# Two-layer kernel in three woven columns: the scan's front moved a batch ahead, the rest's chain reordered

## The chip, the cores and the metric

One core of one Trainium2 chip. The time is the device time of one launch in microseconds, the median of the runs shown.

## What is computed

Two layers of a mixed network on x of 8 batches x 512 tokens x 256 features, in float32. Every part is added to its input.

```python
x = x + scan_layer(layernorm(x))      # state space: in_proj, conv of 4 taps, silu, softplus, 16 states
x = x + ffn_layer(layernorm(x))       # attention only modulates a gated MLP of 1024
x = x + gla_layer(layernorm(x))       # gated linear attention, 4 heads, chunks of 64
x = x + moe_layer(layernorm(x))       # top 4 of 32 experts, inner size 96

# scan_layer, per batch; d over 512 channels, n over 16 states
h, gate = split(z @ in_proj_w); u = silu(conv(h) + b)
dt, B, C = split(u @ x_proj_w); dt, B, C = rms(dt), rms(B), rms(C)
dt = softplus(dt @ dt_proj_w + b)
s[t] = exp(dt[t] * A) * s[t-1] + dt[t] * u[t] * B[t];   y[t] = sum_n s[t] * C[t]
return ((y + u * D) * silu(gate)) @ out_proj_w

# ffn_layer, with its own rms norms of z
mod = 0.1 * tanh(attention(rms(z)) @ A)
g = silu(h @ W_in.T + mod * (h @ A) @ B);  return z + (g * (h @ W_up.T)) @ W_down

# gla_layer
gk = log_sigmoid(z @ Wgk1 @ Wgk2 + b) / 16        # decays, cumulated inside each chunk
o = q_g @ k_g.T (lower triangle) @ v + q_g @ state;  o = o / rms(o) * w * silu(z @ Wg);  return o @ Wo
```

## The kernel before, in words

The kernel is written engine by engine. Each engine has one in-order queue, and parts of the work are generators that yield between small steps. `weave` (line 151) takes steps of two generators in turn, by hand-laid run lengths, the table `ORDER` for batches 0 to 6 and the table `LAST` for the end. So the order of the work on each engine is fixed in the program, and engines meet by semaphores.

**The two columns.** `scan_part(turn, late)` is the whole state-space layer of a batch. `rest_part(turn)` is everything from the feed-forward layer to the linear attention of a batch. `scan_part(t+1)` is woven with `rest_part(t)`. `rest_part(t+1)` starts when the last `out` of `scan_part(t+1)` has been added to `xa`. Routing of the expert layer for batch t-1 (`late_*`) sits inside `scan_part(t+1)`. Before the first rest, `scan_part(0)` runs alone.

**The scan part.** Its front: `x` is loaded into `xa`, statistics (`norm_stats`, line 1292), normalised `xn`, transposed (`T`), projected (`hid`, `gate`), convolved (line 1321: one tap on ACT, three on DVE, from a copy with three zero columns), silu to `u`, `ssm` products, root of sums on POOL, transposes `dtT` and `bcT`, then `dtp` and a softplus from Abs, Relu, Exp and Ln. The B and C rows go to `bc_dram` and come back spread over all partitions, two states a load. After the front 32 units follow (two states of one channel tile each): ACT makes two decays (line 1097), DVE multiplies the drive (`drive_unit`, line 1399), scans (line 1367), multiplies with C (line 1376), and PE sums over the states by transposes (line 2047) into bank 0 or 1. `y_of` adds the skip and the gate, `out` is the output product. All banks of this part are 0 and 1 (ring `A`).

**The rest part.** Statistics of `xa` (`mv0`), POOL makes `rs` and from it `rs2`, ACT writes `nrm` and from it `zn`; transposes `zT`, products `q`, `k`, `v`; 22 score units `S` whose maxima DVE takes (line 1541); maxima transposed (`nmT`) and added to `qT`; 16 score blocks `ST` with their exponentials on ACT (line 1144) and products with v into banks 6 and 7 (`D`); `OT`, `oT`, `mod`, `hA`; eight MLP steps (`mlp_tile`, `down`) with weights streamed into three slots `wslot`, sums in `D`; `add_down`, statistics `mv1`, `gn`, `nT`, then the linear attention: `low`, `gk`, `gq`, `gkey`, `gv`, `gg`, the cumulated decay `cs` (line 1600), `qg`, `kg`, `kd` (line 1614), `kdT`, seven state updates `dS` (lines 1623, 1628), four masked products `AT` (line 1635), four outputs `GO`, sums `g_ss` (line 1640), root on POOL, `goT`, `gout` (line 1657), statistics `mv2`, and `mn`, the rows that are routed. Banks 2 to 5 (ring `B`).

**The end.** Beside the last rest run 40 expert blocks; after it the others and the sums.

## Time and profile before

| | |
|---|---|
| median of 3 runs (lowest, highest) | 3019.35 us (3016.56, 3025.76) |
| span of the profiled execution | 2958.7 us |
| instructions | 36517 |
| PE busy | 2351.0 us (79%) |
| DVE busy | 2163.5 us (73%) |
| ACT busy | 1383.5 us (47%) |
| POOL busy | 575.3 us (19%) |

Busy time is the union of an engine's instructions; where they overlap they are counted once, so that mean durations times counts come out larger. PEclk is the granted clock of TensorE as a share of 2.4 GHz. A line of the busy time by stage or period has the window, its length in us, the busy us and instructions (x) of PE, PE's weight loads, DVE, ACT and POOL, then the granted clock, the DMA engines' busy share and GB/s. A period is the time from one last add of `out` to `xa` (line 1387) to the next.

### The profile page before, as it was taken

The page shows a single profiled execution, that of the slowest core. Times are in us where ns is not written, and L with a number is a line of the kernel's source. Part 1 is how long each engine was busy: PE and PEld are TensorE (multiplying, and loading weights), DVE is VectorE, ACT ScalarE, POOL GpSimd, SP SyncE. Part 2 cuts the span into 40 slices and gives each one's busy share as a digit, 9 for nine tenths or more (in the row PEclk, how much of TensorE's full clock was granted, in tenths as well). Part 3 has the DMA queues.
Part 4 walks back from the last instruction along what each step waited for, and adds up shares of the span by engine and source line. Part 5 has one row for each costly group of instructions (what it writes and reads, how often), then busy time and mean ns, then how long its engine had stood idle before and what let it go on. Part 6 is the DMA issues. An engine that isn't in the chain of part 4 may idle for free. (4 is left out here: it accounts for less than half of the span.)

```text
span 2958.7 us, 36517 instructions
## 1 busy us (share of the span) xinstructions
PE 2351.0 (79%) x12305; PEld 1420.5 (48%) x12305; DVE 2163.5 (73%) x3017; ACT 1383.5 (47%) x2217; POOL 575.3 (19%) x569
## 2 busy tenths in 40 slices
PE   4448896889778977887788869787879688988991
PEld 2335354535453545444544545345535453556880
DVE  4993898489948894899669975998589852246666
ACT  5323654366535663566356634654465424143440
POOL 4000101120131013111311120212120230025661
PEclk8558897899889987998799979998999789988995
DMA  2320231023201321133113311231033182355757
GB/s 105 120 79 8 103 113 57 15 87 128 74 28 60 128 94 35 42 126 107 42 35 109 117 49 42 92 127 56 8 112 121 60 212 97 103 195 174 219 180 302
DMA packets 136229, 292.85 MB, mean 99 GB/s; under 512 B 14288, under 2 KB 79200, under 8 KB 135792
## 3 DMA queue, kind: packets, MB, share of 16 engines
q1 hardware_dynamic: 122224, 251.96, 26.2%
q0 software_dynamic: 13824, 38.55, 3.6%
q8 instruction: 104, 1.70, 0.2%
q14 instruction: 77, 0.63, 0.1%
HBM read 220.91 MB, written 69.54 MB: 98 GB/s over the span
## 5 line engine op out<-in xcount | busy, mean ns | idle before, releaser
L1367 DVE TENSOR_TENSOR_SCAN scan<-scan 128x1024 f32<-128x1024 f32 x256 | 585.9, 2289 | 34.4 <-ACT scan L1097 26.4
L2047 PE MATMUL bank<-ident,scan 128*128 128x128 f32 x2048 | 325.3, 315 | 168.9 <-DVE scan L1376 158.1
L1097 ACT ACTIVATE scan<-scan 128x511 f32<-128x511 f32 x512 | 337.2, 713 | 164.2 <-DVE scan L1367 163.5
L2047 PEld LDWEIGHTS bank<-ident,scan 128*128 128x128 f32 x2048 | 271.6, 162 | 260.1 <-DVE scan L1376 158.4
L1399 DVE TENSOR_TENSOR scan<-scan 128x1024 f32<-128x1024 f32 x256 | 310.5, 1213 | 29.5 <-PE bank L2047 28.5
L1376 DVE TENSOR_TENSOR scan<-scan 128x1024 f32<-128x1024 f32 x256 | 312.0, 1219 | 7.8 <-DVE rest L1579 7.5
L1936 PE MATMUL bank<-hT,wslot 128*128 128x512 f32 x512 | 246.9, 607 | 0.0
L1541 DVE TENSOR_REDUCE rest<-bank 128x2 f32<-128x1024 f32 (+3 forms) x176 | 196.5, 1126 | 66.5 <-PE bank L2118 63.5
L819 POOL DMA_INDIRECT rows_dram<-stage,slot_at x128 | 164.9, 1288 | 370.4 <-DVE scan L1367 313.1
L1144 ACT ACTIVATE rest<-bank 128x2048 f32<-128x2048 f32 (+3 forms) x128 | 158.2, 1236 | 146.7 <-PE bank L2138 146.6
L1936 PE MATMUL bank<-xT,scan 128*128 128x512 f32 (+1 forms) x352 | 185.0, 672 | 7.4 <-ACT xT L983 4.8
L2113 PE MATMUL bank<-rest 32*128 32x384 f32 (+3 forms) x1024 | 185.4, 464 | 2.3 <-DVE rest L1541 1.7
L1321 DVE SCALAR_TENSOR_TENSOR scan<-scan 128x512 f32<-128x512 f32 x96 | 71.9, 752 | 144.9 <-ACT scan L1033 142.4
L983 ACT ACTIVATE scan<-bank 128x512 f32<-128x512 f32 x112 | 65.2, 595 | 230.1 <-PEq L2052 89.5
L1936 PE MATMUL bank<-scan 128*128 128x512 f32 x320 | 153.2, 608 | 3.6 <-ACT scan L983 3.1
L797 POOL TENSOR_SCALAR rs<-mv 128x4 f32<-128x4 f32 x24 | 10.1, 421 | 691.9 <-DVE off L1300 691.9
L1936 PEld LDWEIGHTS bank<-hT,wslot 128*128 128x128 f32 x512 | 88.8, 189 | 115.4 <-issue 108.6
L1923 PE MATMUL bank<-ident,rest 128*128 128x128 f32 x352 | 57.8, 324 | 107.5 <-ACT rest L1110 52.6
L2135 PE MATMUL bank<-causal_t,ident_b 128*128 128x128 bf16 x512 | 54.8, 235 | 105.5 <-ACT rest L1144 67.7
L894 POOL DMA_INDIRECT y_dram<-rest,y_at x120 | 115.1, 959 | 60.6 <-DVE rest L1867 47.5
L2071 PE MATMUL bank<-wslot,rest 128*128 128x256 f32 x512 | 120.4, 380 | 1.0 <-PE bank L2047 0.2
L1163 ACT ACT_TABLE_LOAD x49 | 62.9, 1283 | 120.7 <-PE bank L1936 120.6
(341 smaller groups left out, 4231.2 us busy)
## 6 DMA issues: line engine op xcount, KB each, us to landing
scan<-bc_dram SPq DMA_DIRECT2D x256, 512.0 KB, 3.8
wslot<-wt SPq DMA_DIRECT2D x64, 384.0 KB, 3.5
rows_dram<-pad SPq DMA_DIRECT2D x32, 670.0 KB
scan<-y_dram SPq DMA_DIRECT2D x32, 512.0 KB, 10.1
rest<-rows_dram SPq DMA_DIRECT2D x108, 134.0 KB, 2.5
scan<-rows_dram SPq DMA_DIRECT2D x52, 134.0 KB, 2.7
scan<-wt SPq DMA_DIRECT2D x4, 1536.0 KB, 13.6
xa<-x SPq DMA_DIRECT2D x8, 512.0 KB, 3.8
```

The lines of the kernel that those rows point to most:

```text
L819: g.indirect_dma_start(rows_dram, bass.IndirectOffsetOnAxis(ap=slot_at[:, j:j + 1], axis=0), stage[:, j % NT], None).then_inc(scattered.se ...
L894: g.indirect_dma_start(y_dram, bass.IndirectOffsetOnAxis(ap=y_at[:, b % NYA:b % NYA + 1], axis=0), y[:, n % y.shape[1]], None).then_inc(y_ ...
L1097: i = a.activation(decay[:, unit % 2, n, 1:], dt[:, c, 1:], ACT.Exp, scale=a_neg[:, c, 2 * pair + n:2 * pair + n + 1])
L1144: a.activation(probT[:, u % NPT, :, 0:SEQ - j * P], banks(("ST", u))[:, :, 0:SEQ - j * P], ACT.Exp)\
L1367: d.tensor_tensor_scan(flat, decay[:, unit % 2].rearrange("p n t -> p (n t)"), flat, 0.0, ALU.mult, ALU.add).then_inc(decay_used.sem, 1)
L1376: d.tensor_tensor(drive[:, unit % NDRIVE], drive[:, unit % NDRIVE], bc[:, load % 2, 1], ALU.mult).then_inc(unit_done.sem, 1)
L1399: d.tensor_tensor(drive[:, unit % NDRIVE], dtu[:, c].unsqueeze(1).broadcast_to([P, 2, SEQ]), bc[:, load % 2, 0], ALU.mult).then_inc(drive_ ...
L1541: d.tensor_reduce(nmax[:, t, heads, r].rearrange("p i r -> p r i"), banks(("S", u))[:, :, 0:n * width].rearrange("p r (i k) -> p r i k", i=n),
L1936: m = t_.matmul(b[0:rows, cols], lhsT, rhs, start=(i == 0), stop=(i == len(pairs) - 1))
L2047: m = t_.matmul(A.bank(("yT", c))[:, t * P:(t + 1) * P], drive[:, unit % NDRIVE, n, t * P:(t + 1) * P], ident[:, :], is_transpose=True, st ...
L2071: m = t_.matmul(D[t // 2][:, (t % 2) * HID:(t % 2 + 1) * HID], inner[:, f % 2, t * P:(t + 1) * P], slot[:, 2 * NF * P:], start=(first and ...
L2113: t_.matmul(b[:, k, at:at + width], qT[rows, i, t * P:(t + 1) * P], kT[rows, i, 0:width], start=(i == heads.start), stop=False, skip_group ...
```

## The change

The work of both columns is cut anew into three columns on each engine, `U` (the 32 units and `y`), `R` (the rest), `X` (everything at the side). `weave` takes steps from all three by one long run list per engine. `LAST` goes; `ORDER` covers the whole run up to the last experts.

- The scan's front is split. `front_part(t+2)` (statistics to the first two softplus tiles) is in X and runs beside `units(t+1)` and `rest_part(t)`. `gate_part` has the other two softplus tiles and the gate products. `out_part` has `out`. `tail_part` has `mv2` and `mn`. X is, on PE: out(t), gates(t+1), routing(t-1), front(t+2).
- Front, gates, out and routing use banks 6 and 7 (rings `F`, `G`, `O`, `K`) in turns with the rest, which has them for `D`. The front's `x`, `ssm` and two softplus tiles are in the weight slots, so is the routing's scratch. `handed` waits for the last holder of a bank. x is loaded twice, once for the front and once for the residual.
- `u` of channel tiles 2 and 3 has two places, for odd and even batches. The convolution is done by DVE in place, from PSUM. `y` is formed in `u` and `sgate`.
- In the rest: `rs2` comes straight from the variance and `zn` straight from `xa`; `nrm` and `hT` follow after the first transposes. `Wgk1 @ Wgk2` is folded once at the start, so `low` goes. `hA` and `up` of f = 0 stand before `mod`. `e_kd` and `kd` come before `qg` and `kg`. `dS`, `AT` and `GO` are interleaved as `CHUNK_WORK` says. The root of the sums, and the products with it, go token tile by token tile.

In the DVE list of the changed kernel a middle batch reads so (steps decoded from the run list; t is the rest's batch, the units are those of t+1, C is the product with C):

```
rest: statistics of xa              tail of t-1; units: scans 2-5; xb; drive 6, scan 6, drive 7, C 6
routing of t-1, first half          maxima 0, 1; rank; maxima 2, 3; rank; maxima 4, 5
scan 7 ... C 9 one step between each two maxima up to 21; dtu 2, scan 10; nmT 0-3
units drive 11 ... scan 20, y 0, y 1; OT 0-3; units to C 21; gmod; scan 22
inner 0-3; unit steps with inner 4, 5, 6, 7; scan 27, drive 28
add_down, mv1; front t+2: statistics; units C 27 ... scan 30; front: conv 0, 1; unit; conv 2, 3
cs; scan 31; kd; C 31; qg; kg; y 2; dS 0-2, AT 0; y 3; front: ssm; dS, AT, to AT 3
front: dt 0, dtu 0, dt 1; drive 0 of t+2; dS 6, g_ss 0, 1; dtu 1; out; go; scan 0; ... gout
```

The core of the diff:

```diff
-def weave(rest, scan, runs):
-    for n, part in zip(runs, itertools.cycle((rest, scan))):
-        for _ in range(n):
-            next(part, None)
+def weave(columns, order):
+    for run in order.split():
+        for _ in range(int(run[1:])):
+            next(columns[run[0]], None)
...
+CHUNK_WORK = [("dS", 0), ("dS", 1), ("dS", 2), ("AT", 0), ("dS", 3), ("AT", 1), ("GO", 0), ("dS", 4), ("AT", 2),
+              ("dS", 5), ("AT", 3), ("GO", 1), ("dS", 6), ("GO", 2), ("GO", 3)]
...
+            def front_in(turn):
+                yield
+                if turn >= 2:
+                    sp.wait_ge(down_done.sem, down_done.at(turn - 2, NFT))
...
+                sp.dma_start(x_f, x[turn:turn + 1].rearrange("b (t p) d -> p (b t) d", p=P)).then_inc(x_in.sem, 16)
...
+                    elif f == 0 and in_slots(turn - 1):
+                        sp.wait_ge(lv.sem, lv.named(turn - 1, "routed"))
                     sp.wait_ge(down_done.sem, down_done.at(turn, f - NSLOT + 1 if f >= NSLOT else max(g for g in range(NWT) if g % NSLOT == f) + 1 - NWT))
                     sp.dma_start(wslot[:, f % NSLOT, :], wt[f]).then_inc(w_in[f % NSLOT].sem, 16)
...
+                s = power(rp, turn, rs2[:, :], mv[:, :, 1], 1.0 + 1e-6, 1e-11, NT)
+                pool.wait_ge(rp.sem, rp.at(turn, s))
+                marked("off2", rp.step(g.tensor_tensor(off2[:, :], off[:, :], rs2[:, :], ALU.mult).then_inc(rp.sem, 1)))
...
+                        i = d.scalar_tensor_tensor(tile[:, back:], b[:, 0:SEQ - back], conv_w[:, c, k:k + 1], tile[:, back:], ALU.mult, ALU.add)
...
+            def front_part(turn):
+                yield
+                pe.wait_ge(fa.sem, fa.named(turn, "xn"))
+                if turn >= 2:
+                    pe.wait_ge(d_free.sem, d_free.at(turn - 1, 0))
...
+            def out_part(turn):
+                yield
+                pe.wait_ge(uv.sem, uv.named(turn, f"y{NCT - 1}"))
+                if turn + 1 < BATCH:
+                    handed(F.given_back(turn + 1, ("dtp", 0)), F.given_back(turn + 1, ("dtp", 1)))
...
-                product(B, turn, ("low", 0), [(g_gk1[:, c], xT[:, c]) for c in range(NF)], rows=RANK)
-                yield
-                pe.wait_ge(B.freed_sem(("low", 0)), B.freed_at(turn, ("low", 0)))
-                product(B, turn, ("gk", 0), [(gk2[:, :], lowT[0:RANK, :])])
+                product(B, turn, ("gk", 0), [(g_gkw[:, c], xT[:, c]) for c in range(NF)])
...
+            def side():
+                for turn in range(-1, BATCH):
+                    yield from out_part(turn) if turn >= 0 else idle(IDLE["PE"]["O"])
+                    if turn < BATCH - 1:
+                        yield from gate_part(turn + 1)
+                        yield from late_alone(turn - 1, turn - 1, K) if turn >= 1 else idle(IDLE["PE"]["L"])
+                        yield from front_part(turn + 2) if turn + 2 < BATCH else idle(IDLE["PE"]["F"])
...
+            columns = {
+                "U": itertools.chain.from_iterable(units(turn) for turn in range(BATCH)),
+                "R": itertools.chain(idle(IDLE["PE"]["R"]), *(rest_part(turn) for turn in range(BATCH)), late_alone(0, BATCH - 1, L)),
+                "X": side(),
+            }
+            weave(columns, ORDER["PE"])
```

## Rows read from the trace of the kernel before

**Rows 1.** Busy time by stage of the third rest, 844.3 to 1145.3.

```profile
844.30:884.70 40.40, 32.85 (x120) 19.72 (x120) 12.60 (x38) 19.72 (x37) 5.77 (x12) 0.83 0.04 14
884.70:938.00 53.30, 45.94 (x244) 22.72 (x243) 44.14 (x68) 27.64 (x44) 8.34 (x7) 0.98 0.15 49
938.00:990.00 52.00, 42.67 (x400) 21.08 (x400) 46.51 (x39) 32.37 (x38) 8.87 (x7) 0.89 0.32 110
990.00:1056.70 66.70, 65.57 (x243) 36.23 (x244) 63.69 (x53) 40.97 (x51) 1.14 (x1) 1.00 0.37 127
1056.70:1145.30 88.60, 60.84 (x322) 42.08 (x321) 74.27 (x86) 37.72 (x63) 23.32 (x15) 0.79 0.18 63
```

**Rows 2.** The same view by period, and the last stretch.

```profile
0.00:234.00 234.00, 106.35 (x400) 77.33 (x400) 176.67 (x153) 79.62 (x126) 31.00 (x64) 0.63 0.28 96
234.00:537.00 303.00, 252.03 (x1323) 144.62 (x1324) 232.81 (x243) 159.32 (x234) 29.53 (x28) 0.88 0.21 70
...
844.30:1151.60 307.30, 254.17 (x1352) 147.10 (x1353) 243.94 (x290) 160.49 (x237) 51.17 (x46) 0.89 0.22 76
...
2380.30:2690.00 309.70, 267.68 (x1365) 154.61 (x1366) 118.00 (x332) 105.03 (x193) 60.05 (x68) 0.91 0.52 154
```

**Rows 3.** DVE in order of time, two scan steps: start, us, engine, line.

```profile
404.94 2.29 DVE L1367 TENSOR_TENSOR_SCAN scan<-scan 128x1024 f32<-128x1024 f32 x1 [0.31 <-DVE rest L1579]
...
409.40 2.29 DVE L1367 TENSOR_TENSOR_SCAN scan<-scan 128x1024 f32<-128x1024 f32 x1
```

**Rows 4.** The same view, milestones of the third rest, 856 to 1145 us.

```profile
856.42 1.41 DVE L1294 BATCH_NORM_STATS2 a_stats<-xa 128x6 f32<-128x256 f32 x4 [3.91 <-DMA xa<-x]
...
942.01 0.69 DVE L1351 TENSOR_TENSOR scan<-scan 128x512 f32<-128x512 f32 x1
...
1093.26 0.68 DVE L1614 TENSOR_TENSOR rest<-rest 128x512 f32<-128x512 f32 x1
...
1115.32 1.42 DVE L1635 TENSOR_TENSOR rest<-bank,tri 128x256 f32<-128x256 f32 x4
...
1123.31 0.39 DVE L1640 TENSOR_REDUCE g_ss<-hT 128x4 f32<-128x256 f32 x1
...
1144.64 0.69 DVE L1657 TENSOR_TENSOR xb<-xb,bank 128x512 f32<-128x512 f32 x1 [0.85 <-PE bank L1949]
```

**Rows 5.** All engines, then DVE, in order of time: the first front.

```profile
5.30 1.41 DVE L1294 BATCH_NORM_STATS2 a_stats<-xa 128x6 f32<-128x256 f32 x4 [5.30 <-DMA xa<-x]
...
65.03 2.28 DVE L1399 TENSOR_TENSOR scan<-scan 128x1024 f32<-128x1024 f32 x1
```

**Rows 6.** PE, instructions grouped, 985.1 to 1049.1: busy, mean ns, idle before.

```profile
L1936 PE MATMUL bank<-hT,wslot 128*128 128x512 f32 x58 | 28.0, 607 | 0.0
...
L2071 PE MATMUL bank<-wslot,rest 128*128 128x256 f32 x48 | 11.4, 381 | 0.1
...
L2047 PE MATMUL bank<-ident,scan 128*128 128x128 f32 x88 | 11.0, 273 | 0.1
```

**Rows 7.** The page, costliest groups, whole span.

```profile
L1541 DVE TENSOR_REDUCE rest<-bank 128x2 f32<-128x1024 f32 (+3 forms) x176 | 196.5, 1126 | 66.5 <-PE bank L2118 63.5
...
L1321 DVE SCALAR_TENSOR_TENSOR scan<-scan 128x512 f32<-128x512 f32 x96 | 71.9, 752 | 144.9 <-ACT scan L1033 142.4
...
L1936 PE MATMUL bank<-scan 128*128 128x512 f32 x320 | 153.2, 608 | 3.6 <-ACT scan L983 3.1
```

**Rows 8.** Instructions grouped by line and shape, whole span.

```profile
L1505 DVE SCALAR_TENSOR_TENSOR scan<-scan,bank 128x512 f32<-128x512 f32 x32 | 23.8, 744 | 28.4 <-PE bank L1923 28.4
...
L799 POOL TENSOR_TENSOR rs<-rs,minus_half 128x4 f32<-128x4 f32 x32 | 38.8, 1212 | 2.7
...
L799 POOL TENSOR_TENSOR g_ss<-g_ss,minus_half 128x16 f32<-128x16 f32 x8 | 36.3, 4543 | 0.7
```

**Rows 9.** ACT in order of time, a function table load and what follows.

```profile
1080.47 1.28 ACT L1186 ACT_TABLE_LOAD   x1
1081.77 0.63 ACT L1186 ACTIVATE rest<-rest 128x512 f32<-128x512 f32 x1
```

More of the change, by code:

```diff
@@ L1103, in rest_part @@
                 yield
[L1104 to L1111 removed]
+                act.wait_ge(rp.sem, rp.named(turn, "off2"))
+                marked("zn", normalise(ra, turn, zn, xa, rs2, off2))
                 for c in range(NF):
```

1048 lines of the change are left out of this document (571 added, 477 removed), and 84 rows, old and new, of tables (IDLE, LAST, ORDER).

## The prediction

> **What bounds the kernel now.** I read the busy time by period first. From 234 us on, seven periods of 303 and then 307.2 us follow each other; in each, the attention, MLP and gated linear attention of one batch (the rest) run beside the state-space scan of the next [rows 2]. They make 2146 of the 2958.7 us of the span. In one of them PE is busy 254.1 and DVE 243.9 of 307.2 us, so neither is full, and a better order can give back at most 53 us a period. What is late where is read from the same view cut at the rest's own milestones [rows 1]. I call the stages A (last add to `xa` to first score maximum, 40.4 us), B (maxima, 53.3), C (scores and softmax, 52.0), D (MLP, 66.7) and E (gated linear attention, 88.6); 1145.3 to 1151.6 is a handover of 6.3 us in which the next batch's scan result is still being added. In A the DVE works 12.6 us and sits 28 us, because no scan unit may run before the front (norm, projection, convolution, softplus) of its own batch is done: that front begins with `a_stats` at 856.4 and ends with the last `dtu` at 942.0 [rows 4]. In D both engines are full. In E DVE has 74.3 of 88.6 us, PE 60.8 at a granted clock of 0.79. So DVE's idle time lies in A (28), B (9), E (14) and the handover, and it is there because the 32 units are squeezed into C, D and E.
>
> **Prices.** One scan unit (drive, scan, product with C) costs DVE 4.46 us when units follow each other [rows 3] and PE 1.0 us of transposes at full clock (11.0 us for 88) [rows 6]. The MLP costs PE 80 instructions of 512 columns at 28.0/58 = 0.48 us and 64 of 256 columns at 11.4/48 = 0.24 us, 54 us with the half covered ones counted in full; I take 52. The 40 instructions for hid, gate and softplus inputs cost 153.2/8 = 19.2 us a batch, 7.7 for hid alone [rows 7]. The 22 maxima cost DVE 196.5/8 = 24.6 us a batch [rows 7].
>
> **Stage A and the handover: 46.7 to 40 us.** The new DVE order puts five units (22.3 us), the new tail's statistics and most of the routing behind the statistics of the rest: about 34 us of DVE work, all below the stage's length. The chain stays: statistics, POOL, normalise, transposes, then q, k and v on PE. PE loses hid, 7.7 us, and gets five units' transposes, 5 us. The new `rs2` is computed from the variance itself and not by way of `nrm`: it takes one normalising pass of 2 us off the chain. The residual add of the next batch is no longer in the way, since it falls in E: that takes the handover's 6.3 us, of which I count 4. The zeroing of 128x4096 that POOL used to do at the end now sits before the first maximum; the 40 us of the stage hide it, and uncovered it would cost its 3.5 us. That makes 46.7 - 2 - 4 = 40.7, and 40 with PE's relief. Bounds: 36 (relief counted in full) and 46.7 (none).
>
> **Stage B: 53.3 to 46.** Front work leaves: twelve convolution steps (752 ns each [rows 7], part of them here), the normalising and the softplus sums, some 20 us of DVE. Three units come in, 13.4, and a last scan, 2.3. With maxima 24.6, ranking 3 (sixteen short steps, by their sizes) and the four additions to qT 2.5 the sum is 46, all on DVE, and PE has only 34 us. Bounds 43 and 50.
>
> **Stage C: 52.0 to 51.** Ten units before, ten after (44.6), two y steps and the four OT steps: about 51 on DVE; the exponentials' chain on ACT and PE is as it was. Bounds 50 and 53.
>
> **Stage D: 66.7 to 63.** PE is full at 65.6 of 66.7 us [rows 1]. It keeps the MLP's 52; its units drop from eleven (88 transposes in the slice, eight a unit [rows 6]) to about seven, 4 us less; `hA` and the first `up` go ahead of the wait for `mod`, which I count at nothing since PE hardly waits here. DVE then idles some 24 us here, which the order wastes. Bounds 60 and 66.7. Two new waits stand on SP's queue, with the unit's loads of B and C rows behind both: the first weight load of a batch waits for the routing of the batch before, since routing borrows the weight slots, and the load of x for the front waits for the last `down`. DVE's order ends the routing before the fifth of 22 maxima, some 80 us ahead of the MLP, and weights have 3.5 us to land: nothing. If that cover went, units would stand still for as long as the routing is late.
>
> **Stage E: 88.6 to 86.** Here both signs meet. Gains on the chain: the low-rank product, its eviction and two hand-overs go (3 us, an estimate from two instructions of 0.48, an eviction of 0.6 and waits as long); `e_kd` is asked for first (1.5); states, masked products and outputs are interleaved, where now kd at 1093.3 is followed by 22 us of states until AT at 1115.3 and outputs after that (8); the root of sums is taken tile by tile, so that the last tile waits for a POOL step of 4 elements, 1.2 us, and not of 16, 4.5 us [rows 4, 8] (3). Chain: 88.6 - 15.5 = 73. Load: this stage gets the whole front of batch t+2, the `out` products and the first gates. DVE: 74.3 less four units (17.8), plus twelve convolution steps (8.9) and the front's other sums and the out adds (8), is 73; that the convolution now reads PSUM costs nothing, 744 ns against 752 [rows 7, 8]. PE: 60.8 less 4 for units, plus hid 7.7, softplus inputs 3.8, half of the gates 3.8 and some 14 for the front's small products and `out`, is 86 at the clocks of now; but the 60.8 were run at 0.79, partly at the level of 1.2 GHz behind PE's own gaps, and with these filled I take 75 (no relief at all would be 86 of work and a stage of 97). PE's stalls of 6 before the first transposes and some 5 later give 86. ACT, 37.7 us now [rows 1], gets front, softplus and gates, some fifty activations and two more table loads, 33 more: 71. Four things of 71 to 75 us in one in-order weave do not come out at 75. Bounds: 78 (all hidden) and 100 (a third of the front's 86 us [rows 4] shows, less the chain's gain).
> A rule of the Trainium skill speaks against loading ACT in E. In this trace a switch of function table takes 1.28 us and the next activation starts at once (1080.47 + 1.28, then 1081.8) [rows 9]. The page ScalarE: Activation LUTs, What ACT_TABLE_LOAD costs, says a drain of about 1.38 us comes on top, 2.66 in all; the row shows no such drain. With some nine switches in E the page's price would put ACT at 71 + 12 = 83 and E at about 93; by the row it is 71 and 86.
>
> **The period and the sum.** 40 + 46 + 51 + 63 + 86 = 286 us, 21 less than 307.2. Before the first period: the front alone takes from 5.3 to 65.0 [rows 5]; its gates and half of its softplus leave, 6 us, but the units of batch 0 now share DVE with the front of batch 1, 20 us less 10 that fit in its waits. So the rest of batch 0 begins 4 us later, at 238. The first period has no routing and is 4 us shorter now (303.0) [rows 2]: 282. The seventh has no front beside it: 276. Start of the last rest: 238 + 282 + 5 x 286 + 276 = 2226, now 2380.3. Behind it lie 578.4 us, and of these I take 10 off, since its first 310 us are PE work for 267.7 [rows 2] and only waits can go. Span 2226 + 568 = 2794. The profiled span and the median of the three runs differ by 3019.35 - 2958.7 = 60.65 us outside the span; it stays. 2794 + 60.65 = **2855 us**. (A difference of 0.3%, 9 us, is what a measurement of this kernel can tell from none.)
>
> **Rivals.**
> *The floor.* The stages overlap more than I grant, the period comes to PE's 252 plus 13 of waits, 265: 2855 - 7 x 21 = 2708. For it: PE and DVE are complementary in A, B and E. Against: DVE is given 37 us of work in D's 63 and PE 34 in B's 46. Chance 0.13.
> *E is thick.* ACT or the loaned banks and slots hold E at 100, the period at 300: 2855 + 98 = 2953. For it: four loads over 70 us. Chance 0.18.
> *Slower.* The front of t+2 is on the path of the rest: it can start only when the last `down` has given up its weight slots and PSUM banks, and DVE's order has its `dtu` ahead of the rest's last sums. If it takes 86 us there as it does now [rows 4] after a 4 us load, and 22 us of the rest (from g_ss at 1123.3 to the last gout at 1145.3 [rows 4]) follow, E is 112 and the period 312: 2855 + 7 x 26 = 3037. It decides from a front of 83 us on. Against: alone it takes 60 [rows 5]. Chance 0.09.
> *It does nothing.* The units merely move, DVE's idle time goes from A into D, the period stays at 305 to 309: 3019. Chance 0.04.
> My forecast, period 276 to 297 (2785 to 2932): 0.56.
>
> **How the numbers follow.** Faster 0.13 + 0.18 + 0.56 = 0.87, same 0.04, slower 0.09. The stage bounds summed are 267 and 316 if all go one way; the range takes in the thick E and half of the floor: 2725 to 2965, leaving out about 0.18.
>
> **What would show it.** Periods by the distance between last adds to `xa`: 286. A with DVE busy over 30 us; B DVE-bound; D with DVE under 45 of 63 us; E 86 with PE clock above 0.9; the front inside E under 65 us; ACT table loads 19 to 22 a period. Wrong would be: an E over 100, a rest that waits for `handed` banks or for weights behind the routing, or a scan unit that waits for its decay.

## The result, and the profile after

| | before | changed |
|---|---|---|
| median (lowest to highest) | 3022.56 us (3016.56 to 3031.03, 4 runs) | 3062.66 us (3051.84 to 3072.32, 4 runs) |
| ratio, 95% interval | | 1.0126 [1.0096, 1.0157] |
| span of the profiled execution | 2958.7 us | 3049.8 us |
| its own time | | 3051.84 us |

The change makes the kernel 1.3% slower where I forecast 2855 us, 5.5% faster, in a range that ended at 2965. Everything below is about these 200 us.

First the changed kernel by period, in the columns of [rows 2]. The first line ends where the statistics of the first rest begin, the others end at the same point of the next rest, the last five cut the last rest and the experts:

```profile
0.00:253.60 253.60, 131.78 (x479) 90.98 (x479) 201.85 (x184) 123.05 (x181) 41.96 (x67) 0.68 0.31 108
253.60:554.00 300.40, 263.61 (x1340) 150.00 (x1340) 237.59 (x247) 172.32 (x247) 43.19 (x33) 0.89 0.20 67
...
859.40:1166.50 307.10, 271.34 (x1352) 155.05 (x1350) 242.74 (x292) 154.08 (x230) 67.12 (x51) 0.86 0.23 78
...
2077.80:2382.10 304.30, 257.57 (x1260) 148.86 (x1258) 213.94 (x251) 112.59 (x170) 58.38 (x42) 0.82 0.22 74
2382.10:2500.00 117.90, 95.07 (x453) 49.11 (x454) 52.35 (x129) 33.05 (x54) 30.02 (x36) 0.81 0.65 172
2500.00:2611.00 111.00, 94.07 (x465) 44.86 (x465) 18.19 (x49) 40.63 (x48) 5.19 (x6) 0.95 0.17 55
2611.00:2686.00 75.00, 59.48 (x270) 43.25 (x271) 28.76 (x112) 23.95 (x66) 27.86 (x31) 0.86 0.81 268
2686.00:2800.00 114.00, 73.09 (x306) 50.72 (x305) 43.49 (x139) 28.64 (x60) 29.45 (x36) 0.64 0.21 64
2800.00:3049.00 249.00, 180.97 (x986) 141.52 (x984) 154.75 (x473) 65.55 (x218) 108.02 (x113) 0.88 0.64 214
```

Seven periods of 300.4, 305.4, 307.1, 298.9, 305.4, 307.0 and 304.3 us stand where 306.1 and 307.2 stood (the window of the first in [rows 2] starts 2.4 us behind the last add, which ends at 231.6, so that it shows 303): nearly nothing was gained. DVE does the work it did (242.7 us a period, 243.9 in [rows 2]). PE is busy 271.3 us for 254.2, at a lower granted clock, 0.86 for 0.89. And the last rest with the experts takes 667.7 us.

The third rest by its stages A to E, as in [rows 1]:

```profile
859.40:899.50 40.10, 34.76 (x161) 22.39 (x160) 34.93 (x62) 25.38 (x45) 19.09 (x15) 0.91 0.32 105
899.50:955.80 56.30, 51.26 (x194) 22.62 (x192) 45.54 (x49) 5.34 (x8) 7.17 (x6) 0.58 0.17 62
955.80:1017.30 61.50, 48.29 (x405) 25.02 (x406) 50.63 (x43) 34.92 (x42) 15.31 (x5) 0.81 0.30 99
1017.30:1082.30 65.00, 65.00 (x237) 35.80 (x235) 40.36 (x35) 28.63 (x35) 3.04 (x3) 0.99 0.29 95
1082.30:1166.50 84.20, 72.03 (x362) 49.21 (x361) 71.28 (x107) 59.81 (x100) 22.51 (x22) 0.94 0.13 48
```

A, D and E are what was forecast: DVE works 34.9 us in A where it had 12.6 (I said 34), PE is full in D and DVE has 40.4 of 65 us there (I said under 45), E is 84.2 us with PE at 72 and a clock of 0.94 (I said 86 and 75). B and C are the failure, 10 us each. In B DVE's 45.5 us are those of the forecast (46), but PE is busy 51.3 of 56.3 us at a clock of 0.58; it was 0.98 before. In C DVE's 50.6 us are again those of the forecast (51), but it sits idle for another 10.9. Over the period DVE's idle time is 64.4 us, it was 63.4; it has left A (28 us before, 5 now) for D (3 before, 25 now).

What PE does in B, grouped (line, engine, operation, shapes, count, busy us, mean ns, idle before), before and then changed:

```profile
L2113 PE MATMUL bank<-rest 32*128 32x256 f32 (+3 forms) x112 | 22.0, 490 | 0.3 <-DVE rest L1541 0.3
L1936 PE MATMUL bank<-scan 128*128 128x512 f32 x28 | 13.1, 597 | 0.3 <-ACT scan L983 0.3
L2118 PE MATMUL bank<-causal,ident_b 128*128 128x128 bf16 (+2 forms) x43 | 7.1, 245 | 0.0
L1949 PE MATMUL bank<-scan 128*128 128x160 f32 x32 | 4.6, 301 | 0.0
```

```profile
L2330 PE MATMUL bank<-rest 32*128 32x256 f32 (+3 forms) x112 | 37.1, 775 | 2.2 <-DVE rest L1717 2.2
L2335 PE MATMUL bank<-causal,ident_b 128*128 128x128 bf16 (+2 forms) x42 | 8.9, 312 | 0.0
```

The same 112 score products cost 22.0 us before and 37.1 now. What stood between them, the products of the front and the gates (L1936, L1949, 17.7 us), is what the change moved out, most of it into E. Less work in the stage, and more time on the engine.

The waits in C, DVE in order of time:

```profile
1002.24 0.75 DVE L1680 SCALAR_TENSOR_TENSOR scan<-scan,bank 128x512 f32<-128x512 f32 x1 [6.59 <-PE bank L2115]
...
1014.01 0.26 DVE L1732 RECIPROCAL prob_sum<-bank 128x16 f32<-128x16 f32 x1 [3.64 <-PE bank L2115]
```

y1 (the second y step) waits 6.59 us for PE and the first OT step 3.64: 10.2 of the 10.9 us.

In the last rest the linear attention's chain stops from about 2611 to 2686: the lists of PE, DVE, ACT and POOL have 25 expert blocks in one run between its first two transposes. The DMA engines are busy 0.81 of these 75 us, and the 114 us after them have a PE clock of 0.64 with little beside the chain.

### The profile page after: what moved, and what is told of

Same layout as the page of the kernel before. It is cut to its first block and busy times, and to the rows that moved or that the text cites. A ratio compares the mean times of both kernels' runs of the same rounds, so it can differ in the third digit from the quotient of the medians.

```text
span 3049.8 us, 36680 instructions
## 1 busy us (share of the span) xinstructions
PE 2495.4 (82%) x12295; PEld 1486.0 (49%) x12295; DVE 2162.5 (71%) x3033; ACT 1368.1 (45%) x2184; POOL 676.4 (22%) x609
## 5 line engine op out<-in xcount | busy, mean ns | idle before, releaser
L967 POOL DMA_INDIRECT rows_dram<-stage,slot_at x128 | 196.7, 1536 | 1103.8 <-DVE scan L1561 845.7
L2255 PEld LDWEIGHTS bank<-ident,scan 128*128 128x128 f32 x2048 | 283.3, 165 | 200.1 <-DVE scan L1570 130.3
L1585 DVE TENSOR_TENSOR scan<-scan 128x1024 f32<-128x1024 f32 x256 | 319.6, 1248 | 17.9 <-PE bank L2255 16.2
L1570 DVE TENSOR_TENSOR scan<-scan 128x1024 f32<-128x1024 f32 x256 | 318.6, 1244 | 0.0
L2330 PE MATMUL bank<-rest 32*128 32x384 f32 (+3 forms) x1024 | 288.0, 677 | 15.6 <-DVE rest L1717 15.4
L1327 ACT ACTIVATE rest<-bank 128x2048 f32<-128x2048 f32 (+3 forms) x128 | 157.3, 1229 | 99.9 <-PE bank L2356 99.8
L1752 DVE TENSOR_TENSOR rest<-rest,bank 128x512 f32<-128x512 f32 x64 | 44.0, 687 | 197.6 <-PE bank L2128 156.3
L2128 PE MATMUL bank<-xT,scan 128*128 128x512 f32 x320 | 149.9, 614 | 3.9 <-ACT xT L1295 3.4
L2330 PEld LDWEIGHTS bank<-rest 32*128 32x128 f32 x1024 | 103.1, 247 | 65.3 <-issue 34.8
L2141 PE MATMUL bank<-scan,xT 128*128 128x256 f32 x512 | 120.4, 392 | 4.2 <-ACT xT L1151 4.2
L2356 PE MATMUL bank<-rest 32*128 32x512 f32 (+3 forms) x1024 | 120.8, 545 | 0.0
L2371 PE MATMUL bank<-rest 128*32 128x512 f32 (+3 forms) x1024 | 105.6, 488 | 16.1 <-ACT rest L1327 16.1
```

The lines of the kernel that those rows point to most:

```text
L967: g.indirect_dma_start(rows_dram, bass.IndirectOffsetOnAxis(ap=slot_at[:, j:j + 1], axis=0), stage[:, j % NT], None).then_inc(scattered.se ...
L1327: a.activation(probT[:, u % NPT, :, 0:SEQ - j * P], banks(("ST", u))[:, :, 0:SEQ - j * P], ACT.Exp)\
L1570: d.tensor_tensor(drive[:, unit % NDRIVE], drive[:, unit % NDRIVE], bc[:, load % 2, 1], ALU.mult).then_inc(unit_done.sem, 1)
L1585: d.tensor_tensor(drive[:, unit % NDRIVE], dtu[:, c].unsqueeze(1).broadcast_to([P, 2, SEQ]), bc[:, load % 2, 0], ALU.mult).then_inc(drive_ ...
L2128: m = t_.matmul(b[0:rows, cols], lhsT, rhs, start=(i == 0), stop=(i == len(pairs) - 1))
L2255: m = t_.matmul(A.bank(("yT", c))[:, t * P:(t + 1) * P], drive[:, unit % NDRIVE, n, t * P:(t + 1) * P], ident[:, :], is_transpose=True, st ...
```

## The experiments

Kernels of one group ran on one chip beside the kernel before, and each ratio is to before on that chip; chips differ (first experiments), so medians are only compared inside a group. The groups are: b0, t_even, b_fill, c_shift (before: 2967.37 us); a1, f_half1, f_bf1, c_shift3 (3027.25); b1, g_only, t_d, g_d (3024.35); g_d2, c_exp, c_exp2, g_fill (3024.33); c_pe, c_pe_fill (3028.01). Rests are counted from 0 where they have a number: rest 2 is the third. Stage lengths are from each profile by the milestones used above. "Order only" means that the programmed order of steps on the engines' lists changed and no instruction.

### 1. Does a fixed 60 us lie outside the span, and is the result stable?

Three kernels without an edit.

> The kernel before, unchanged, to see where its time lies beside the changed one. The prediction took the 60.65 us between the profiled span (2958.7) and the median (3019.35) as lying outside the span. If that holds, a new profile has a span near 2959 at a time near 3020. The rival: the profiled execution was a quick one, nearly nothing lies outside the span (the changed kernel's profile has 3049.8 of 3051.84 us), and the timed executions have a span of about 3015; then the new profile shows in which stretch they are longer. The last rest is the first suspect, since the periods up to 2380 us end within 1 us of each other in the two traces.

> The changed kernel unchanged, for its time and profile beside the others on one chip. Its first profile has rest starts at 253.6 and 2382.1 and an end at 3049.8 us; with only the last blocks spread its last rest was 64 us shorter (2984.2). If the two agree on everything else, its time is near 3045 here, with the time from the last add_down to g_ss of the last rest at 108 us. Rival: executions differ by as much as the changes, and it is near 3010.

> The kernel before once more, beside the others. On one chip it took 2967 us, on another 3027, and nearly all of each is span. The changed kernel's periods are the same on both (298.8 to 307.1), its last rest with the experts is not: 599 to 627 us on the one, 645 to 668 on the other. So, if the chip here is of the slow kind, this profile has starts of the rests as before up to 2381 and an end at 3015 to 3030; if of the quick kind, it ends near 2957.

| | median, us | before, same chip | ratio [95%] | profiled span |
|---|---|---|---|---|
| b0 (before) | 2971.68 | 2967.37 | 1.0014 [0.9993, 1.0035] | 2956.3 at a time of 2958.17 |
| a1 (changed) | 3053.02 | 3027.25 | 1.0077 [1.0049, 1.0105] | 3057.3 |
| b1 (before) | 3026.13 | 3024.35 | 0.9999 [0.9978, 1.0019] | 3027.4 |

The span ends about 2 us short of the time in each of them. My 60.65 us "outside the span" are then the distance between two chips: the profile of before agrees with b0's stage by stage to 0.6 us, so it came from a chip like that one, and the median from one like b1's. Where it lies is seen in b0 and b1, the same program: middle periods are 307.2 us in both, while B of the last rest and the expert stretch are not (windows of b0, then of b1).

```profile
2420.00:2463.50 43.50, 41.11 (x238) 20.18 (x236) 31.00 (x43) 4.43 (x13) 18.39 (x20) 1.00 0.53 168
...
2690.00:2955.00 265.00, 197.77 (x1113) 160.01 (x1111) 171.34 (x556) 76.75 (x242) 135.35 (x141) 0.87 0.67 225
```

```profile
2433.60:2500.30 66.70, 51.57 (x236) 23.84 (x236) 31.36 (x44) 4.93 (x13) 18.14 (x19) 0.74 0.33 108
...
2728.00:3025.00 297.00, 211.77 (x1109) 164.67 (x1108) 173.55 (x555) 72.60 (x241) 134.28 (x140) 0.84 0.60 199
```

23 us in B, where the clock was 1.00 and then 0.74, and 32 us at the end, where the DMA engines moved 225 and then 199 GB/s; 14 more lie in the first period (320.2 us for 306.1). Why the chips differ stays open. The changed kernel is slower than before in both comparisons, by 1.3 and 0.8%.

### 2. The last rest

t_even: order only, changed kernel, last rest. t_d: t_even, and blocks 4 to 11 as well.

```diff
 PE, DVE, ACT, POOL, last rest
-nT0, expert blocks 12 to 36 in one run, nT1, ... gout
+nT0, nT1, expert blocks 12 to 39 a few at a time between the steps gk ... gout          (t_even)
-scores and exponentials with expert blocks 4 to 11 between them, MLP
+scores and exponentials, MLP with expert blocks 4 to 11 between its steps               (t_d)
```

> The changed kernel, with only the order behind the last MLP changed: in it 25 expert blocks stand in one run between the first and the second transpose of nT of the last rest, on PE, DVE, ACT and POOL (2611 to 2686 us of its trace, where the chain of the rest stands still); here they stand one or two at a time beside the steps of the chain. Theory (the run of blocks stands in the chain's way): g_ss of the last rest comes some 60 us sooner than 2717, the end with it, about 3000 us. Rival (the stretch is set by the DMA engines, which are at 0.9 to 1.0 of their time between 2618 and 2668, so the same bytes take as long wherever the blocks stand): less than 15 us, 3050.

> The last blocks spread, and besides, expert blocks 4 to 11 moved out of the last rest's stage C, where one stands beside each score block, into its MLP, with SP's row loads behind the weight loads that would wait for them. C of the last rest was 70 us with them and 51.7 in the kernel before; each block is a chain of six hand-overs between PE, ACT and DVE in the chain of exponentials. Theory: C falls to 52 to 55, D grows from 59.6 by the blocks' PE work, 5 to 8: 10 us less than the run with the last blocks spread alone. Rival (PE and ACT are busy enough in C, 49.8 and 44.8 of 70 us, that the blocks are no loss there): no difference.

t_even: 2996.29 us, ratio 1.0101 [1.0071, 1.0132]; its middle periods are those of the changed kernel to 0.3 us, and statistics to g_ss in the last rest takes 77.8 us (108.4), 31 us less where I had expected 60. From the last add to `xa` to the end it takes 603.8 us; c_shift, on the same chip and with the order of the changed kernel there, takes 622.2. So spreading the blocks gains 18 us, since part of what the chain wins is spent in the experts behind it; the ratio alone does not show it (1.0126 and 1.0077 for the changed kernel). t_d: 3029.13 us, ratio 1.0026 [1.0007, 1.0044]. The same stretch takes 645.5 us in t_d; on the same chip it is 670.6 in g_only (below), which keeps the order of the changed kernel there, and 633.1 in before (b1). In t_d the scores' stage C is 46.4 us without blocks in it (70 with them), D is 73.4 for 59.6. So the order of the last rest cost some 37 us against before, and 25 of them come back by order alone.

### 3. B: too much work, or PE at half clock?

These kernels put an extra product ahead of each of the 22 score units, into the same bank; the score product that follows starts the bank anew, so its result is overwritten. b_fill: changed kernel. f_half1 and f_bf1: t_even.

```diff
                     width = (t + 1) * P
+                    t_.matmul(b[:, 0, :], ident[:, :], xT[:, 0], start=True, stop=True, skip_group_check=True)     # b_fill, 512 columns f32
+                    # f_half1: the same with 256 columns
+                    # f_bf1: ident_b, causal (four times side by side), 512 columns bf16
                     for i in range(heads.start, heads.stop):
```

> The changed kernel with one more product per score unit (128 rows, 512 columns, its result overwritten at once by the unit's own), 22 more a batch, about 10 us of PE work at full clock. In the trace of the changed kernel TensorE's clock falls to 1.2 GHz some 7 us after the first maximum and stays there to the last, and PE is busy 46.8 of the stage's 50.4 us. Theory (the stage is slow because PE has too little to do in it, the clock falls, and PE at half clock bounds it): with more work the clock stays up in the stage, DVE bounds it, and the stage falls from 50.4 to 43 to 46 us: seven times 5, about 3030 us. Rival (the clock falls for another reason, or the stage is DVE's): the added work costs its price at half clock, 22 x 0.86 = 19 us a batch less what hides, 3130 to 3190 us.

> The last blocks spread, as above, and the extra product of each score unit with 256 columns instead of 512: about 11 us of PE work a batch where the 512 columns took 22.3 us in 50, hid wholly, and kept the clock at 1.0 in stage B. Theory (B is bound by PE at 1.2 GHz, and by PE's added work once the clock is up): the clock stays up, PE has 28.7 + 11 + 4 = 44 us, DVE 43.6, B goes from 54.7 to about 48 us, the period to 297: 2996 less seven times 6 is 2950. Rival (B is bound by the hand-over between PE and DVE, whatever the clock): B stays at 54, 2996.

> The same with one bf16 product of 512 columns per score unit instead (the mask's own kind, some 0.22 us at full clock, 5 us a batch). Theory: if so little keeps the clock up, B is DVE's and falls to 46 to 47 us, 2940; if it does not, the clock falls as without it and B is 54.7 plus what the product costs at half clock, 57 to 59: about 3015.

b_fill: 3002.77 us, ratio 1.0135 [1.0096, 1.0173]. f_half1: 3065.31, 1.0102 [1.0053, 1.0151]; its trace is that of the longest of four executions, 3106.10 us, which the ratio leaves out (the others took 3041.50 to 3070.98). f_bf1: 3067.08, 1.0114 [1.0074, 1.0154]. None gained what was expected of it. Stage B of the third rest in b_fill, then f_half1, then f_bf1:

```profile
898.80:953.50 54.70, 49.55 (x236) 20.65 (x234) 45.23 (x49) 5.33 (x8) 6.85 (x6) 1.00 0.18 63
```

```profile
912.70:980.70 68.00, 63.66 (x236) 30.68 (x234) 45.68 (x49) 5.35 (x8) 7.53 (x6) 0.62 0.16 52
```

```profile
904.70:964.90 60.20, 55.46 (x215) 24.29 (x214) 45.56 (x49) 5.34 (x8) 5.89 (x6) 0.63 0.17 57
```

The largest addition costs nothing (B 54.7 us, it was 53.4 to 56.6), because the clock is then 1.00; but B did not fall to the 43 to 46 us that I had expected. Half of it costs 12 us at 0.62, in five rests; in the fifth rest of the same f_half1 the clock stayed at 1.00, and B was 48.4 us with exactly the same instructions:

```profile
1546.40:1594.80 48.40, 41.06 (x236) 20.76 (x234) 44.96 (x49) 5.35 (x8) 7.52 (x6) 1.00 0.21 73
```

So B has two courses, and the granted clock decides: work was not what made B long. Both stand in one execution, so its length does not matter here. In the changed kernel the clock fell in the second rest at about 599 us, at the end of a gap in PE's work (PE in order of time, then the two stretches around it by window):

```profile
596.54 0.39 PE L2335 MATMUL bank<-causal,ident_b 128*128 128x256 bf16 x2
598.59 1.65 PE L2330 MATMUL bank<-rest 32*128 32x256 f32 x6 [1.65 <-DVE rest L1717]
```

```profile
553.00:598.00 45.00, 38.78 (x197) 25.11 (x197) 39.77 (x71) 24.88 (x44) 19.04 (x14) 0.92 0.29 94
598.00:648.00 50.00, 46.99 (x156) 20.07 (x156) 39.34 (x39) 5.06 (x8) 6.67 (x6) 0.52 0.19 69
```

In the third rest it falls at 905.8 us, behind the same gap, and comes back at about 954; so the 0.58 of that stage is 48 us at the lower level. But the gap alone does not decide. The fourth and the fifth rest of f_half1 have the same first 16.2 us of B, with the same two gaps of 0.79 and 1.28 us, all at a clock of 1.00:

```profile
1230.10:1246.30 16.20, 14.13 (x92) 7.67 (x91) 14.51 (x21) 1.34 (x2) 5.60 (x4) 1.00 0.30 100
1546.40:1562.60 16.20, 14.12 (x93) 7.69 (x91) 14.51 (x21) 1.34 (x2) 5.61 (x4) 1.00 0.29 99
1246.30:1298.10 51.80, 49.56 (x146) 23.02 (x145) 31.18 (x29) 4.01 (x6) 1.92 (x2) 0.51 0.11 37
1562.60:1594.80 32.20, 26.94 (x146) 13.07 (x144) 30.46 (x29) 4.01 (x6) 1.91 (x2) 0.99 0.17 60
```

Then the clock falls in the one and stays in the other. What decides between the courses stays open; that 256 columns a unit do not hold the clock, as I had expected, is what f_half1 shows.

### 4. B: the gates put back

g_only: changed kernel, with the four gate products and their silus of the next batch again between the score units, behind the routing. g_d: g_only and t_d.

```diff
 PE, rests 1 to 6 (ACT: silus behind v1 and two pairs of decays)
-out, dtp 2 3, gate 0-3, routing, front | S0 ... S21
+out, dtp 2 3, routing, ... | S0 S1 gate0 S2-4 gate1 S5-7 gate2 S8-11 gate3 S12 ... S21
```

> The changed kernel with one part of it undone, for rests 1 to 6: the four gate products of the next batch (16 instructions of 512 columns, 7.7 us at full clock) go back in between the score units, behind the routing, with their silus on ACT. The extra product of 256 columns per score unit, which did nothing, made B 48.4 us in the one period in which the clock stayed up and 68.2 in the five in which it fell. Theory (what left B is what kept TensorE at 2.4 GHz there): with the gates B has 40 us of PE work at full clock, and 44 of DVE; with the clock up it falls from 53 to 56 to about 48 us, and A and E lose PE work, 2 us together: periods 295. If the clock falls all the same, B is 45 + 15 + 7 = 67 us or less, since the gates cost double then, and the period 315.

> All three: gates between the score units, the last blocks spread, blocks 4 to 11 in the MLP. If the theories hold, the changed kernel less 7 x 8 for the clock in B, less 20 to 60 for the last blocks, less 10: under the kernel before by 1 to 2%, on either chip. If the clock falls in B with the gates there, it is slower than the kernel before.

g_only: 3046.39 us, ratio 1.0088 [1.0057, 1.0119]. g_d: 3014.84, 0.9975 [0.9952, 0.9997], where I had expected 1 to 2% under before. B of rests 1 to 5 sums to 263.2 us in g_d and 278.2 in t_d, on the same chip: 15 us, and the medians are 14.3 apart. The third and the fourth rest of g_d:

```profile
891.50:940.00 48.50, 40.52 (x210) 19.64 (x208) 44.64 (x49) 15.43 (x18) 6.75 (x6) 0.93 0.20 72
...
1189.10:1243.50 54.40, 48.42 (x210) 22.30 (x208) 45.13 (x49) 15.44 (x18) 6.76 (x6) 0.78 0.19 65
```

With 16 products more in the stage B is shorter, 48.5 us where the clock holds best; in four of the rests 1 to 6 it is still 54.4 to 56.2. Only the gates were put back, not the front's products.

g_d2 is g_d again on another chip, and g_fill adds f_bf1's product to it.

> The kernel of g_d unchanged, so that what is added to it here has its own base on this chip. Expected: 0.995 to 0.9995 of before, C of a middle rest 58 to 62 us, B 48.5 to 54.5.

> g_d with one more bf16 product of 512 columns ahead of every score unit (its result is overwritten), about 5 us of PE work at full clock a batch. In g_d stage B was 48.5 us where the granted clock was high and 54.4 where it was not. Theory 'the clock of B is what is left': 128-row products between the scores keep it at 2.4 GHz, B is 48 to 51 in every rest, the time 8 to 20 us shorter than g_d2. Rival 'the added work counts': B grows by up to 5 us, as it did in f_bf1 (60.2 us at a clock of 0.63), the time 10 to 25 us longer.

g_d2: 3015.58 us, ratio 0.9968 [0.9949, 0.9986]. g_fill: 2995.39, 0.9911 [0.9884, 0.9937], 20 us less. B of the rests 1 to 6 is 50.8, 50.5, 50.8, 50.5, 51.4 and 50.8 us (48.5 to 56.7 in g_d2). The product that had made B 60.2 us in f_bf1 saves time here: with the gates it is enough to hold the clock.

### 5. C: DVE's sum, the decays, or PE's list?

c_shift: changed kernel, order only; four units leave C for the waits of the MLP. c_shift3: c_shift, and on SP the weight loads w3 and w4 go ahead of two units' loads.

```diff
 DVE (ACT's decays and PE's transposes likewise), rests 1 to 5
-... drive 18, C 17, y 0, scan 18, ... y 1, scan 19, ... scan 20, OT 0-3, ... inner 0, inner 1 ...
+... OT 0-3, drive 18, C 17, y 0, scan 18, drive 19, ... gmod, C 18, y 1, inner 0, scan 19, ... inner 1, scan 20 ...
 SP (c_shift3)
-B12 C12, w3, w4
+w3, w4, B12 C12
```

> The changed kernel with three scan units (the last product of unit 17 to the scan of 20) moved from ahead of OT into the waits of the MLP, on DVE, with their decays on ACT and transposes on PE, in rests 1 to 5. Stage C (last maximum to first OT on DVE) took 64.2 us in the changed kernel against 51 predicted, and DVE sat 25 us idle in D. Theory (C is as long as the units that stand in it, and ACT's exponentials go one by one behind the decays): C falls by about 13 us, D grows by 3 to 5 for the transposes on a full PE, the period from 307 to 297 or less: five times 8 to 10, about 3018 us. Rival (C is set by the chain of exponentials between ACT and PE, not by the units): C falls by less than 4 and D grows by as much, 3060 us or more.

> The three units moved from C into D once more, and the fourth and fifth weight loads of the MLP moved ahead of the unit loads that now wait longer on SP's queue. In the run without that, C fell by 4.7 us only, since DVE then sat 20.7 us before OT (the chain of exponentials between ACT and PE takes 52 us by itself), and D grew by 15, of which 10.6 were one wait of PE for a weight load queued on SP behind a unit's C rows. Theory (that queue was D's loss): D comes to 68 to 70, C stays at 56 to 57, the period is 304 to 306, the same as without the shift: near the changed kernel's own time. Rival (ACT's table switches between exponential and silu, now sixteen in D, hold D up): D stays at 75 or more.

c_shift: 3075.57 us, ratio 1.0376 [1.0298, 1.0454]. c_shift3: 3072.46, 1.0150 [1.0128, 1.0173]. C fell to 56 us only (13 had been expected off it), and DVE waited 20.7 us in it for OT; D grew to 80 us, 71 in c_shift3. So units were not what held C. The 9 us of D between the two are SP's in-order queue: PE waited for a weight load that stood behind the loads of moved units (c_shift, PE in order of time):

```profile
1059.31 3.40 PE L2292 MATMUL bank<-hT,wslot 128*128 128x512 f32 x4 [10.58 <-DMA wslot<-wt]
```

ACT in C of the changed kernel waits seven times, 10.8 us in all, for a scan of DVE before a pair of decays; five of these waits are of 1.6 to 2.7 us. c_exp and c_exp2 move the decays later:

```diff
 ACT, rests 1 to 6, d = pair of decays, P = exponential       (on g_d)
-P0 d13 P1 d14 P2 d15 P3 d16 P4 yT0 d17 P5 P6 P7 P8 yT1 d18 d19 P9 d20 P10 P11
+P0 P1 d13 P2 P3 d14 P4 d15 P5 d16 yT0 P6 P7 d17 P8 yT1 d18 d19 P9 d20 P10 P11            (c_exp)
+... P8 yT1 P9 d18 P10 P11 d19 d20                                                        (c_exp2)
```

> g_d with another order on ACT alone, rests 1 to 6: in C each pair of decays stands one or two exponentials later (d13 behind exponential 1, d14 behind 3, d15 behind 4, d16 and the eviction yT0 behind 5, d17 behind 7; now one pair stands between every two). Theory 'decays hold up the exponentials': now ACT waits 1.6 to 2.7 us five times in C for a scan of DVE before a pair of decays, with a ready exponential behind it, and four exponentials take 18.1 us where they took 12.3 in the kernel before. Then C falls by 4 to 6 us, the time by 20 to 35 us against g_d2. Rival 'twelve units are C': DVE has 50 us of work in C and now waits for the decays instead; C stays within 1 us, the time within 6 us.

> c_exp, and in addition d18 behind exponential 9, d19 and d20 behind exponential 11. Now a double pair (2.55 us) stands ahead of exponential 9, and exponentials 8 to 12 take 14.3 us against 10.9 in the kernel before. Theory of the decays: C another 2 to 3 us shorter than in c_exp, by 12 to 18 us in the time. Rival: the scans behind y1 now wait for their decays and C and D together are unchanged or longer by up to 3 us.

c_exp: 3036.35 us, ratio 1.0040 [1.0023, 1.0057], 21 us more than g_d2 and C 62 to 64 us. c_exp2: 3006.73, 0.9938 [0.9916, 0.9961], 9 us less, C 58.9 to 61.4. Moving the decays alone did not do it: C did not fall by 4 to 6 us. ACT's waits for scans fell from 10.8 to 3.4 us in C of the third rest, but its waits for score blocks rose from 12.0 to 22.4. c_exp's trace shows what holds the exponentials now (PE, then ACT, in order of time):

```profile
1268.87 1.09 PE L2266 MATMUL bank<-ident,scan 128*128 128x128 f32 x8 [2.52 <-DVE scan L1577]
1273.33 1.97 PE L2266 MATMUL bank<-ident,scan 128*128 128x128 f32 x8 [3.36 <-DVE scan L1577]
```

```profile
1277.75 1.45 ACT L1334 ACTIVATE rest<-bank 128x1536 f32<-128x1536 f32 x1 [9.54 <-PE bank L2367]
```

PE's list has the transposes of units 12, 13 and 14 in one run before score block 5. PE waits there for DVE, unit after unit at 4.46 us, and the score blocks and exponentials wait behind it. Then the blocks that had piled up stand in front of the transposes that y1 needs, and DVE waits. In the changed kernel the run is there too (eight transposes a unit, so 24 for three), but PE does not wait in it; there ACT's waits for scans delay the exponentials instead:

```profile
974.55 3.05 PE L2255 MATMUL bank<-ident,scan 128*128 128x128 f32 x24
```

The kernel before has no such run between its score blocks: there the units' transposes come eight at a time. c_pe breaks the run up on top of c_exp2; c_pe_fill adds the product of g_fill.

```diff
 PE, rests 1 to 6, u = transposes of a unit         (on c_exp2; yT0 on ACT behind P7)
-ST4 PV3, u12 u13 u14, ST5, PV4, ST6 PV5, ST7 PV6, ST8 PV7, u15 y0, ST9, PV8, ST10 PV9, ST11 PV10, ST12 PV11, y1 u16
+ST4 PV3, u12, ST5, PV4, ST6 PV5, u13, ST7 PV6, u14, ST8 PV7, u15 y0, ST9, PV8, ST10 PV9, y1, ST11 PV10, ST12 PV11, u16
```

> c_exp2 with another order on PE (and yT0 on ACT behind exponential 7), rests 1 to 6: in C the transposes of units 12, 13 and 14 stood in one run between score blocks 4 and 5; now 12 stands there, 13 behind block 6 and 14 behind block 7; the transposes that y1 waits for go ahead by two score blocks. Theory 'the score blocks wait in PE's list for the units': in c_exp PE waited 2.5 and 3.4 us at these transposes for DVE's products with C, and ACT 9.5 us for the score block behind them. Then four exponentials take 12 to 14 us there, C falls from 58.9 to 61.4 in c_exp2 to 52 to 56 us, by 15 to 35 us in the time; DVE keeps under 3 us of waits in C besides that for OT. Rival 'DVE's own sum is C': DVE has 50 us of work in C and waits 3.6 us for OT whatever the order, so C is 57 or more and the time is within 8 us of c_exp2.

> c_pe and g_fill together: the order of c_pe and one bf16 product of 512 columns (its result is overwritten) ahead of each score unit. The two causes lie in different stages, C and B, so the gains should add: g_fill's 20 us against g_d2 and c_exp2's 9 us give 2987, and what c_pe gains over c_exp2 comes on top; B 50 to 51.5 us in rests 1 to 6. Rival 'the clock ties them': a shorter C moves where PE's gaps fall, B loses its clock and the gain of the fill in some rests; the time is then that of c_pe, within 8 us.

| | median, us | before, same chip | ratio [95%] | periods 2 to 6 |
|---|---|---|---|---|
| c_pe | 2962.66 | 3028.01 | 0.9793 [0.9773, 0.9813] | 290.2, 290.1, 290.2, 290.1, 292.9 |
| c_pe_fill | 2956.39 | 3028.01 | 0.9767 [0.9749, 0.9784] | 291.9, 291.9, 292.4, 291.2, 290.2 |

Stages B and C of the third rest in c_pe:

```profile
878.50:927.00 48.50, 40.57 (x210) 19.73 (x210) 44.63 (x49) 15.43 (x18) 6.73 (x6) 0.93 0.21 72
927.00:981.20 54.20, 42.49 (x416) 21.90 (x416) 50.61 (x44) 34.89 (x42) 15.28 (x5) 0.97 0.33 113
```

C is 54.2 us in all of rests 1 to 6 with the same 50.6 us of DVE work: of the 10.9 us of idle time 3.6 are left, 2.95 of them before OT. On top of c_exp2, three changed places in PE's list and yT0 are worth 5 to 7 us a rest. PE's clock in C is not the reason: at the same 0.94 C is 58.9 us in c_exp2 and 54.2 in c_pe_fill.

```profile
952.30:1011.20 58.90, 42.88 (x416) 22.66 (x416) 50.92 (x44) 34.57 (x42) 12.04 (x5) 0.94 0.30 104
1230.70:1284.90 54.20, 43.27 (x416) 22.20 (x416) 50.61 (x44) 34.91 (x42) 15.29 (x5) 0.94 0.33 113
```

PE's new list with ACT's old one was not run, so how the gain divides between the two lists is not shown. B is 48.5 us in four of the six rests (in one of them in c_exp2), though nothing in B was changed: c_pe gained 44 us on c_exp2 by the ratios, more than I had expected of C (15 to 35); between the two profiles C of rests 1 to 6 is 35 us shorter and B 23. The two remedies do not add up, as the rival of that run had it: c_pe_fill is 6 us below c_pe and not 20, since B's clock already holds in most rests of c_pe, and there the added product costs 2 us a rest (50.5 to 52.6 us for 48.5). Both versions beat the kernel before, by 2.1 and 2.3%.

## Why the prediction was wrong

The terms of my sum against the profiled execution of the changed kernel, in us:

| term | forecast | measured | miss |
|---|---|---|---|
| start of the first rest | 238 | 253.6 | +15.6 |
| first period | 282 | 300.4 | +18.4 |
| five periods | 1430 | 1523.8 | +93.8 |
| seventh period | 276 | 304.3 | +28.3 |
| last rest to the end | 568 | 667.7 | +99.7 |
| outside the span | 60.65 | 2.0 | -58.6 |
| time | 2855 | 3051.8 | +197 |

*Right.* Stage A (40, measured 38.6 to 40.1), D (63, 63.6 to 65.0), E (86, 84.0 to 84.2), with their loads as above; the front inside E takes 63.8 us from its statistics at 1084.6 to the end of its last `dtu` at 1148.4 (I said under 65); ACT table loads are 19 a period (19 to 22). The handover is gone. The rival that ended slower, with the front on the rest's path in E, did not happen, nor did the thick E: the kernel became slower by other mechanisms than the one I had named. Nearest came the rival to which I gave 0.04, "it does nothing": four of the five middle periods are 305.4 to 307.1 us, and DVE's idle time did go from A into D. But that is not why they are long, since it stands in D as well in c_pe, where they are 290.

*The table loads.* The switches cost 1.28 us each in E, with the next activation at once:

```profile
1138.20 1.28 ACT L1226 ACT_TABLE_LOAD   x1
1139.50 0.63 ACT L1226 ACTIVATE wslot<-wslot 128x512 f32<-128x512 f32 x1
```

By the page ScalarE: Activation LUTs of the Trainium skill, What ACT_TABLE_LOAD costs, a drain of about 1.38 us comes on top; neither this trace nor the length of E shows it; the trace has 8 loads in E, where I had taken nine. ACT has 59.8 us in E, less even than my 71.

*B, 46 forecast, 53.4 to 56.6 measured.* The step "all on DVE, and PE has only 34 us" failed. DVE's sum was right to 0.5 us. The 34 us of PE were priced at full clock, and I took away the very products that had stood between the score products, without asking at what clock PE would then run. I did ask this of E, where the gaps are visible in [rows 1]; B had 0.98 there and I took it as given. That the clock makes B long is shown by f_half1 (48.4 and 68 us with the same instructions); that products between the scores hold it, by b_fill, g_d and g_fill, though g_d does not in every rest. Worth about 8 to 10 us a period; with the clock held B is 48.5.

*C, 51 forecast, 58.9 to 61.5 measured.* The step "the exponentials' chain on ACT and PE is as it was" failed. DVE's sum was again right (50.6). But the chain shares PE's and ACT's in-order lists with the units, and the run lists had been rewritten. I had decoded the list of DVE and not those of PE and ACT: on ACT decays stand before exponentials and wait for DVE's scans, 10.8 us in C, and on PE three units' transposes stand in one run before a score block. Shown by c_pe, with both lists in a new order, in which C becomes 54.2; c_shift and c_exp had ruled out the units' sum and the decays alone, and PE's list alone is not tested. For every stage I compared the load of engines and took the larger; the waits that each hands the next around a ring of three in-order lists were in neither number.

*The last rest, "I take 10 off".* It rested on the statement that only waits can go, and none was counted as coming. I had not read where the run lists put the expert blocks. On chips where before takes 3024 to 3027 us, before has 633.1 us from the last add to `xa` to the end, and the kernels with the new order there 667.7 to 672.6 (the changed kernel, a1, g_only): 35 to 40 us from the order, of which t_d wins back 25. Another 55 us of the 99.7 are the difference of the chips, 633.1 for 577.7 in before, and the last 10 are those I took off. The 55 are of the same 60 that I had carried as a constant outside the span and that the profile of before did not have in its last stretch: the two errors cancel nearly, -58.6 and +55. That they cancel is luck.

*The start, 4 us forecast, 22 measured (231.6 to 253.6).* "20 less 10 that fit in its waits": beside the units there are nearly no waits to fit in. DVE is busy 99.6 of 100 us from 60 to 160 us, and it was 99.8 of 100 in before. It has 201.9 us of work before the first rest, 25 more than [rows 2] show. [Rows 2] end the start at 234, where the last add had ended at 231.6; so the first period of before was 306.1 us and not 303, and I took 3 us too many off it.

*First and seventh period.* They carry the misses of B and C. Beyond these the seventh (304.3, its E 93.2 us) gains nothing from having no front beside it: behind the rest's last sum at 2366 the last y and `out` of the scan part end at 2382, a handover of 16 us that the front's absence doesn't shorten.

The floor rival said 265 us a period; the best period seen is 290.1, with A 38.8, B 48.5, C 54.2, D 63.3 and E 85.3. That is 4 us from the 286 I had forecast for the change as it stood: the sum over DVE and PE was a fair price for a version with other lists, and not for this order.

## What to carry to other kernels

When work is moved off TensorE, look at the granted clock of the stretch it leaves: what remains can take longer than all of it did before. When a woven order is cut anew, decode the lists of all engines around every chain and look for runs of one column in front of another's step, since a sum of loads per stage says nothing of a ring of in-order lists that wait for each other. And compare the time of the profiled execution itself with its span before any distance between a median and a span is carried as a constant.

## What the runs showed of the hardware

- The same instructions in the same execution took 48.4 us at a granted clock of 1.00 and 68.0 at 0.62 (f_half1, stage B), with the same first 16.2 us at 1.00. In the changed kernel PE was busy in 91% of B, and yet the granted clock was 0.58 over its 56.3 us, 48 of them at the lower of the two levels (0.5, 1.2 GHz); there PE was busy 45.07 of 47 us:

```profile
906.00:953.00 47.00, 45.07 (x146) 18.50 (x144) 36.68 (x35) 4.00 (x6) 6.22 (x5) 0.50 0.20 72
```

- With a 512-column product added to every unit the clock was 1.00 and the stage no longer than without (54.7 us, b_fill).
- Chips differ by 2% for one program (2967 and 3024 to 3028 us), in stretches with heavy DMA traffic or where the clock can take either course; the middle periods are 307.2 us in both profiles (b0, b1).
